# Second MoE layer: adding weighted results to a DRAM table of tokens instead of storing them apart and summing at the end

## The reference

```
t = _to_tokens(x)                                # 16384 tokens x 128
t = t + _L1_ffn_ref(_ln_t(t), gate_w, w1, b1, w2, b2)
x = _from_tokens(t, x)                           # back to channels first

# _L1_ffn_ref: N = 16384, E = 8 experts, K = 2, C = 2560 places per expert
probs = softmax(xf @ gate_w.T);  topk_vals, topk_idx = top_k(probs, 2)
topk_vals = topk_vals / topk_vals.sum(-1)
flat_e = topk_idx.reshape(N * K)
pos = cumsum(onehot(flat_e))[..., flat_e] - 1;   keep = pos < C
expert_in = tokens placed at (flat_e, pos), those beyond C dropped
h = gelu(expert_in @ w1 + b1);  expert_out = h @ w2 + b2
w = topk_vals * keep
out = (expert_out[flat_e, pos] * w).reshape(N, 2, D).sum(axis=1)
```

## Time and profile before

| | |
|---|---|
| median of 3 runs | 2171.72 us |
| profiled execution, its own time | 2161.24 us |
| span of the profiled execution | 2159.5 us |
| busy in the span: PE / DVE / ACT / POOL | 81% / 55% / 36% / 42% |
| granted clock of PE over the span | 0.909 of full |
| queue q1 (SP's loads and stores) | 194.56 MB, 35.7% of 16 DMA engines |
| queue q0 (POOL's indirect DMAs) | 55.89 MB, 8.5% |
| POOL's gathers, line 692 | x160, mean 1012 ns |
| POOL's stores, line 706 | x160, mean 997 ns |

### The profile page before, as it was taken

How to read it: one execution, slowest core, us unless ns; L and a number is a source line. 1 busy time by engine, 2 the same in 40 slices (tenths; PEclk the granted TensorE clock), 3 DMA queues, 4 the chain that set the end, 5 groups by cost and what they waited for, 6 DMA issues and landing times.

```text
span 2159.5 us, 36665 instructions
## 1 busy us (share of the span) xinstructions
PE 1750.2 (81%) x10475; PEld 1478.0 (68%) x10475; DVE 1187.9 (55%) x4407; ACT 772.6 (36%) x1691; POOL 903.1 (42%) x935
## 2 busy tenths in 40 slices
PE   4989996999699999999999946891868777777823
PEld 3777775777588999999988836891855554555512
DVE  4455667556656554677768864678951111111166
ACT  0322331233144444555555531030853332322212
POOL 2000002554267777777744440000026776767610
PEclk9999998999899999999999978995988998999955
DMA  3063566445567886666656654731001222222177
GB/s 120 21 117 86 87 108 124 98 100 102 115 161 189 211 204 177 202 212 211 196 172 187 189 151 86 141 116 82 1 18 46 61 60 56 59 57 60 44 241 233
DMA packets 256135, 264.60 MB, mean 123 GB/s; under 512 B 69236, under 2 KB 224301, under 8 KB 254810
## 3 DMA queue, kind: packets, MB, share of 16 engines
q1 hardware_dynamic: 193754, 194.56, 35.7%
q0 software_dynamic: 28416, 55.89, 8.5%
q10 hardware_dynamic: 33792, 12.06, 2.1%
HBM read 167.37 MB, written 89.67 MB: 119 GB/s over the span
## 4 chain that ended last, share of the span: by engine, by line
PE 58%; DVE 15%; DMA 8%; issue 8%; POOL 5%; ACT 3%; SPq 1%; DVEq 1%; POOLq 0%; ACTq 0%
PE zp L743 9%; PE tp L891 7%; PE tp L901 4%; PE gp L1070 4%; PE zp L1041 3%; PE gp L913 3%; PE zp L913 3%; DMA out<-arena 3%; PE tp L1054 3%; PE tp L823 2%; PE gp L838 2%; DMA arena<-table,arena 2%; POOL arena L692 2%; PE zp L901 2%; POOL results L706 2%
## 5 line engine op out<-in xcount | busy, mean ns | idle before, releaser
L623 POOL DMA_INDIRECT slots<-arena x256 | 256.8, 1003 | 520.1 <-DVE arena L1595 376.0
L664 POOL DMA_INDIRECT results<-arena x304 | 302.3, 994 | 173.2 <-DVE arena L1673 114.6
L692 POOL DMA_INDIRECT arena<-table,arena x160 | 161.9, 1012 | 354.3 <-DVE arena L1838 305.9
L743 PE MATMUL zp<-arena 128*128 128x256 f32 x1024 | 243.3, 393 | 45.8 <-ACT arena L1105 45.5
L743 PEld LDWEIGHTS zp<-arena 128*128 128x128 f32 x1024 | 198.0, 197 | 76.2 <-ACT arena L1105 47.8
L891 PE MATMUL tp<-arena 128*128 128x256 f32 x912 | 222.1, 380 | 0.7 <-issue 0.7
L1673 DVE SCALAR_TENSOR_TENSOR arena<-tp,arena 128x256 f32<-128x256 f32 x304 | 134.5, 481 | 130.8 <-PE tp L901 105.7
L706 POOL DMA_INDIRECT results<-arena x160 | 159.6, 997 | 87.0 <-DVE arena L1863 44.2
L1192 ACT ACTIVATE arena<-tp 128x512 f32<-128x512 f32 x152 | 90.9, 598 | 267.5 <-PE tp L891 265.2
L1305 ACT ACTIVATE arena<-tp,arena 128x512 f32<-128x512 f32 x160 | 109.9, 687 | 192.6 <-PE tp L1054 192.6
L1863 DVE TENSOR_TENSOR arena<-zp,arena 128x512 f32<-128x512 f32 x40 | 27.7, 692 | 271.1 <-PE zp L1041 271.1
(11 more groups left out here) (287 smaller groups left out, 3356.7 us busy)
## 6 DMA issues: line engine op xcount, KB each, us to landing
arena<-in_L_ffn_W SPq DMA_DIRECT2D x304, 192.0 KB
arena<-results SPq DMA_DIRECT2D x56, 512.0 KB, 5.0
arena<-slots SPq DMA_DIRECT2D x152, 134.0 KB
arena<-taps SPq DMA_DIRECT2D x64, 224.0 KB, 4.6
table<-arena SPq DMA_DIRECT2D x4, 2144.0 KB
arena<-in_x SPq DMA_DIRECT2D x8, 1024.0 KB, 9.1
arena<-arena SPq DMA_DIRECT2D x128, 64.0 KB
arena<-in_x SPq DMA_DIRECT2D x16, 512.0 KB, 11.4
```

The lines of the kernel that those rows point to most:

```text
L623: g.indirect_dma_start(slots[r], bass.IndirectOffsetOnAxis(ap=slot[:, k, blk:blk + 1].bitcast(U32), axis=0), rows[:, blk, :], None, bounds ...
L664: g.indirect_dma_start(results, bass.IndirectOffsetOnAxis(ap=row_at[:, q:q + 1].bitcast(U32), axis=0), y_tiles[:, q, :], None, bounds_chec ...
L692: g.indirect_dma_start(quad_in[m][:, q, :], None, table, bass.IndirectOffsetOnAxis(ap=token_at[:, tile:tile + 1].bitcast(U32), axis=0), bo ...
L743: t.matmul(dst, wg[:, j, k, :], xs[c][:, :, k, 0:P], start=(k == 0), stop=False)
```

## The change

A DRAM tensor `total` (16384 rows of 128 values) takes the place of `results` in the second layer. SP fills it with the tokens themselves. For each quad DVE works out each row's weight (`quad_w`, from `W0` and `DW` of the gathered row and from `choice`, the lowest bit of `result_at`), multiplies the biased result by it, and POOL stores it by an indirect DMA that adds to the destination row. Because a token can be met again by another expert, POOL waits, before the first add of every expert but the first, until all adds so far have landed. The last stage loads `total` only; DVE does nothing in it. `table` is written in two halves, after the weights are known. Gathers run four quads ahead.

```diff
-GATHERS_AHEAD = 3
+GATHERS_AHEAD = 4
-        result_at, token_at = arena.take(E8 * CT), arena.take(E8 * CT)
+        token_at, choice = arena.take(E8 * CT), arena.take(E8 * CT)
-        y_fin = [arena.take(KB // 2, 2, P) for _ in range(FIN_RING)]
-        fin = [arena.take(KB // 2, P) for _ in range(2)]
+        quad_w = arena.take(CT // QT, QT)
+        fin = [arena.take(KB // 2, P) for _ in range(FIN_RING)]
# SP
-            for turn in range(NBLK // TURN4):
-                sp.wait_ge(sem("norm4_ready"), turn + 1)
-                part = slice(TURN4 * turn, TURN4 * turn + TURN4)
+            by_place = total.rearrange("(p k) c -> p k c", p=P)
+            for h in range(2):
+                part = slice(GB * h, GB * h + GB)
+                sp.dma_start(by_place[:, part, :], xt[:, part, :]).then_inc(sem("total_out"), 16)
+            for h in range(2):
+                part = slice(GB * h, GB * h + GB)
+                sp.wait_ge(sem("slots_ready"), GROUPS + h + 1)
                 sp.dma_start(table.rearrange(...)[:, part, :], rows[:, part, :]).then_inc(sem("table_out"), 16)
...
+            def load_total(n, j):
+                sp.dma_start(fin[j], by_place[:, bass.ds(KC * n, KC), :]).then_inc(sem(FIN_SEMS[j][0]), 16)
             for j in range(FIN_RING):
-                load_results(y_fin, FIN_SEMS[j][0], j, j)
+                load_total(j, j)
             with sp.Fori(1, NBLK // 4 // FIN_RING) as turn:
                 for j in range(FIN_RING):
-                    sp.wait_ge(sem("fin_ready"), FIN_RING * (turn - 1) + j + 1)
-                    load_results(y_fin, FIN_SEMS[j][0], FIN_RING * turn + j, j)
+                    sp.wait_ge(sem("fin_t_done"), FIN_RING * (turn - 1) + j + 1)
+                    load_total(FIN_RING * turn + j, j)
# GpSimd
             for Q in range(E8 * per):
                 if Q + GATHERS_AHEAD < E8 * per:
                     gather(Q + GATHERS_AHEAD)
+                if Q % per == 0 and Q:
+                    for m in range(per):
+                        pool.wait_ge(sem(f"yq_out{m}"), 64 * (Q // per))
                 pool.wait_ge(sem("yq_ready"), Q + 1)
                 for q in range(QT):
                     tile = QT * Q + q
-                    g.indirect_dma_start(results, ...result_at[:, tile:tile + 1]..., y_quad[Q % 2][:, q, :], None,
-                                         bounds_check=2 * TOKENS - 1, oob_is_err=False
+                    g.indirect_dma_start(total, ...token_at[:, tile:tile + 1]..., y_quad[Q % 2][:, q, :], None,
+                                         bounds_check=TOKENS - 1, oob_is_err=False, compute_op=ALU.add
                                          ).then_inc(sem(f"yq_out{Q % per}"), 16)
# TensorE, last stage: loops over 4 buffers, waits for the load itself
-                for u in range(2):
-                    pe.wait_ge(sem("fin_ready"), 2 * turn + u + 1)
+                for j in range(FIN_RING):
+                    pe.wait_ge(sem(FIN_SEMS[j][0]), 16 * (turn + 1 + FIN_SEMS[j][1]))
...
# VectorE, routing part 7
+                    o.step(v.tensor_copy(rows[:, half, W0], weight[:, 0, half]))
+                    o.step(v.tensor_tensor(rows[:, half, DW], weight[:, 1, half], weight[:, 0, half], ALU.subtract))
# VectorE, after the one-hots
-            o.link(v.tensor_scalar(result_at.bitcast(I32), here, -1.0, None, ALU.add))
+            row = here.bitcast(I32)
+            o.link(v.tensor_scalar(row, here, -1.0, None, ALU.add))
+            v.tensor_scalar(token_at.bitcast(I32), row, 1, None, ALU.arith_shift_right).then_inc(sem("index_ready"), 1)
+            o.link(v.tensor_scalar(row, row, 1, None, ALU.bitwise_and))
+            o.link(v.tensor_copy(choice, row))
# VectorE, quad_norm: ahead of and behind the four normalising instructions
+                weights = quad_w[:, m, :]
+                v.tensor_tensor(weights, quad_in[m][:, :, DW], choice[:, bass.ds(QT * Q, QT)], ALU.mult).then_inc(sem("quad_w_step"), 1)
...
+                dve.wait_ge(sem("quad_w_step"), 2 * Q + 1)
+                v.tensor_tensor(weights, weights, quad_in[m][:, :, W0], ALU.add).then_inc(sem("quad_w_step"), 1)
# VectorE, last_bias: behind the bias
-                                    ).then_inc(sem("yq_ready"), 1)
+                                    ).then_inc(sem("sums_done"), 1)
+                    dve.wait_ge(sem("sums_done"), Q + 2)
+                    dve.wait_ge(sem("quad_w_step"), 2 * Q + 2)
+                    v.tensor_tensor(y_quad[u], y_quad[u], quad_w[:, n % per, :].rearrange("p (q c) -> p q c", c=1)
+                                    .to_broadcast([P, QT, P]), ALU.mult).then_inc(sem("yq_ready"), 1)
-            def final_sum(turn, j):
...
```

More of the change, by code:

```diff
@@ L319, in metaformer @@
         table = scratch("table", TOKENS, ROW_W)
+        total = scratch("total", TOKENS, P)
         results = scratch("results", 2 * TOKENS, P)
@@ L705, in _ @@
                     tile = QT * Q + q
[L706 to L707 removed]
+                    g.indirect_dma_start(total, bass.IndirectOffsetOnAxis(ap=token_at[:, tile:tile + 1].bitcast(U32), axis=0),
+                                         y_quad[Q % 2][:, q, :], None, bounds_check=TOKENS - 1, oob_is_err=False, compute_op=ALU.add
                                          ).then_inc(sem(f"yq_out{Q % per}"), 16)
@@ L1800, in router @@
                 o.link(last)
-                v.scalar_tensor_tensor(out=rows[:, blks, SHIFT], in0=mean_r, scalar=-1.0, in1=rows[:, blks, RSTD],
-                                       op0=ALU.mult, op1=ALU.mult).then_inc(sem("norm4_ready"), 1)
-                dve.wait_ge(sem("norm4_ready"), turn + 1)
+                o.link(v.scalar_tensor_tensor(out=rows[:, blks, SHIFT], in0=mean_r, scalar=-1.0, in1=rows[:, blks, RSTD],
+                                              op0=ALU.mult, op1=ALU.mult))
                 lg = logits[:, blks, :]
```

48 lines of the change are left out of this document (12 added, 36 removed).

## The result

The changed kernel takes 2195.47 us (median of 4 runs, 2194.75 to 2199.46) where the kernel before takes 2172.16 beside it (2169.54 to 2173.91). The ratio is 1.0112, 95% interval 1.0095 to 1.013: slower. The forecast was 2107 us and faster, so it was wrong by the sign.

A forecast was written before the change was run, and what follows sets the result against it. The prediction took POOL's indirect DMAs (10.45 us per quad) to bound the quads and DMA to be 86% busy in the last stage. Routing +0.8, quads -34.2 and last stage -31.1 sum to -64.5: 2107 us, range 2095 to 2225.

The forecast's parts named there:

- the price of the nearest row: Quads, POOL: an add costs the same 1.0 us as a plain indirect DMA, so 0 extra.
- half a second set of descriptors: Quads, POOL: a dearer add at +0.49 us each, giving 2185 us; a full set gives 2264.
- Rival 1: Line 719, POOL: adds cost more; 0.1 to 0.38 us extra 10%, around 0.40 2%, above (slower) 28%.
- Routing: Before the first gather: four added DVE instructions, +0.8 us; the copies to DRAM hidden, cost 0.
- Quads, lead and start: Quads: first add at 1628.9, 0.9 us later; lead of four breaks the circle of waits, last gather 37.5 us earlier.
- the forecast's stage: Whole quads stage: -37.5 us to the last gather and +3.3 after it, together -34.2 us.
- The lead's worth: Quads: four quads of gathers ahead end POOL's waits, so POOL alone sets 10.45 us per quad.
- The multiply: Quads, DVE: 0.9 us more makes PE's quad 8.65 us, still below POOL's 10.45, so hidden.
- Rival 3: Quads: DVE's multiply blocks POOL 0.69 us in each of 40 blocks, +28 us, 2135; 10% together with two other rivals.
- The boundary waits: Quads, 7 expert boundaries: adds have 6.5 us to land, plain stores need at most 3.6; cost 0.
- Quads, end: Last gather to first load of the last stage: 32.9 us by PE's path instead of 29.6, +3.3.
- Last stage: Half the loads: 1.95 us per chunk at 86% DMA share, 68.0 us against 99.05, -31.1 us.

The follow-up runs named there:

- g3: Changed kernel with adds of all 128 rows but only 64 of the 128 words of each; add 1566 ns, quads 519.5 us.
- e1: Changed kernel with its adding stores made plain stores, everything else kept; 2397.5 us, ratio 1.0066 to the kernel before.
- h2: Changed kernel, unchanged, beside the kernel before on a chip where TensorE's results come late; ratio 0.9998.
- g1: Changed kernel whose adds take only 64 of the 128 rows of each tile; add 1401 ns, quads 494.6 us.
- g2: Changed kernel with plain stores of only 64 of the 128 rows; store 907 ns, quads 547.5 us.
- e3: Changed kernel with gathers three quads ahead instead of four; ratio 1.0052 to the kernel before, quads 543.7 us.
- e2: Kernel before with gathers four quads ahead instead of three, nothing else; ratio 1.0026, no difference.
- f2: Kernel before with gathers four quads ahead, the same edit as e2, repeated on another chip; ratio 1.0015.
- the first comparison: Changed kernel beside the kernel before, both unedited, the main measurement; 2195.47 against 2172.16 us, ratio 1.0112.
- g4: Changed kernel with plain stores and without the multiply by the weights on VectorE; quads 502.9 us.
- f4: Changed kernel with four instead of two output buffers in the last stage; 2353.9 us, ratio 0.9902 to the kernel before.

## Why the prediction was wrong

**Which step failed.** "I take 0, the price of the nearest row": the add costs POOL 0.587 us more than the plain store, 93.9 us over 160. The working had said that this number decides the sign, put the break-even at 0.40, and priced half a second set of descriptors at +0.49 for 2185 us. With 0.587 its own formula gives 2107 + 94 = 2201; measured 2195. Rival 1 is what happened; the time lies inside the stated range (2095 to 2225) because that rival had set its upper end. The error was to weigh three rows that agree as evidence on a fourth operation that none of them shows. They say that bytes and direction don't matter, and g3 confirms the bytes for adds. They could not say what an instruction costs that names its destination twice. A chance of 28% for the price past 0.40 was too low with bounds of 0 and 0.98 and nothing between them; it should have been near one half.

The rule that was weighed against the change says that an accumulating DMA reads its destination and writes it later (the Trainium skill, "DMA: Bandwidth & Descriptors", section on rules for kernel authors). 144 packets instead of 32 and 3.3 us to land instead of 2.3 would fit it, but no view shows the read itself: the pages of e1 and h2, with plain stores and with adds, count the same 158.98 MB read from HBM. Of what an add costs GpSimd more than a store, most doesn't grow with the rows, by the split of g1 and g2.

**Routing.** +0.8 forecast, +0.7 measured. The first gather starts at 1603.0, so the copies to DRAM were hidden.

**Quads, lead and start.** The first add starts at 1629.7 (1628.9 plus the late start of 0.7). Put the true prices into the forecast's stage, -34.2 + 93.9 for the adds + 4.2 for the gathers, and it gives +63.9; measured +60.9. So the terms other than the price come out within 3 us together; singly they are not tested by it, since a full POOL covers what the others get wrong. The direct mark, "no wait of POOL for the bias between quads 2 and 35", holds: the waits are 0.3 us at most, 2.1 us in all, 7 times. That shows less than it was meant to, since a POOL that needs 12.85 us a quad would seldom wait with a lead of four or more; with three it did in e3, whose quads are 22 us longer. The lead's worth with plain stores (34 us by the forecast) is measured only on chips where TensorE's results are late, and is nothing there (e2, f2). In the condition of the first comparison it stays open.

**The multiply.** "Hidden" was right of POOL's waits in the changed kernel: 2.1 us in all. With plain stores and late results it costs 36 to 40 us (g4).

Rival 3, the multiply holding GpSimd up, happened, and it is small. It depends on which of the two begins first. In the quad above the gather at 1810.31 begins ahead of the multiply at 1810.49 and takes its 0.99 us. The other order, in the changed kernel and then in e1:

```profile
1720.23 0.69 DVE L1888 TENSOR_TENSOR arena<-arena 128x512 f32<-128x512 f32 x1
1720.33 2.09 POOL L719 DMA_INDIRECT total<-arena  x1 [0.30 <-issue]
```

```profile
2310.35 0.69 DVE L1888 TENSOR_TENSOR arena<-arena 128x512 f32<-128x512 f32 x1
2310.47 1.42 POOL L719 DMA_INDIRECT total<-arena  x1 [0.31 <-issue]
```

The first add of a quad takes 1.63 us as a rule, this one 2.09, and the plain store 1.42 instead of 0.98. In the changed kernel's quads 20 indirect DMAs begin while a multiply runs. Where 0.15 us of it or more are left (14 times), the DMA takes longer than the median of its place in the quad, by what is left less about 0.13 us (0.46 more with 0.59 left, 0.23 more with 0.36 left). The multiply itself always takes 0.69. The bias, which reads PSUM, does nothing of the kind: before, a gather that began with 0.58 us of it left took 1.01 us. All 14 together are 2.3 us, where the rival had set 28 for all 40 multiplies; 1.9 of them lie in the gathers and are part of their +4.2. The trace agrees here with the rule that was cited for it, that a DVE instruction with two inputs in SBUF contends with a GpSimd instruction that reads SBUF (the Trainium skill, "SBUF — State Buffer", "Who interferes with whom"): issuing an indirect DMA behaves like such an instruction when it begins second.

**The boundary waits.** Cost 0, right: adds land within 4.8 us and 6.5 were there. DMA waits ahead of gathers are 0.3 us, once. A version without these waits would race and was not tried.

**Quads, end.** +3.3 forecast, +10.6 measured. From the last gather at 2081.9 to the last add at 2118.7 some 20 adds follow each other at 1.87 us: POOL sets the end too, where the forecast had PE's way. It is the same mis-sized price.

**Last stage.** -31.1 forecast, -28.0 measured, by 2.06 us per chunk instead of 1.95. The forecast took the engines' share, 86%, over from a stage with bigger loads; here it is 80%, and the ring of two was the limit (f4). It had named this limit and set it at stores landing within 3.1 us; they land in 3.5.

**What stays open.** Why TensorE's results reach the others late on some chips, where the 10 us between profile and median lie, and what f4 takes in the condition of the first comparison. An estimate for the last: 1.0112 of 2172 less the 19 us of its last stage (73.8 - 54.7) is about 2177, 5 us above the kernel before.

## What to carry to other kernels

An operation that no row of the trace shows has no price from its neighbours: where an engine without slack issues it some hundred times and the sign hangs on it, treat both bounds as live, or measure one instruction of it first. Before giving work to the engine that sets the pace, divide the gain by the number of its instructions; here 64.5 us over 160 left 0.40 us for each. And a ring of two buffers in front of a DMA that lands after 3.5 us is a limit of its own: two more buffers in the last stage gave 19 us here (f4 against h2).

## What the runs showed of the hardware

- An accumulating indirect DMA of 128 rows keeps GpSimd 1567 ns, a plain one 988; of 64 rows 1401 and 907. Halving the bytes of a row changes nothing (1566).
- It makes 144 packets instead of 32 (80 with 64 rows) and lands in 3.3 us instead of 2.3, with 512 bytes a row. Gathers beside adds become 0.03 us dearer to issue.
- An indirect DMA that GpSimd begins while a DVE instruction with two inputs in SBUF runs takes longer by about what is left of that instruction less 0.13 us (2.09 instead of 1.63 us, 1.42 instead of 0.98). Begun first, it takes its usual time.
- On some chips the same program takes a tenth longer, with DVE and ACT beginning up to some 4 us after the modelled end of TensorE's product, while GpSimd's instruction times stay the same. A change can then measure 1.0112 in one condition and 0.9998 in the other.
- Loads and stores in 2 KB pieces reached 363 GB/s together with four output buffers, and 247 with two.
